# Layer 1's experts: second product feature-major with a gated input; layer 0's first loads on two queues

## What is computed

```python
raw_gate = jax.nn.softmax(x @ gate, axis=-1)                 # 16 experts
gate_topk = top 3 of raw_gate, divided by their sum           # 0 elsewhere
hidden = relu(einsum('btd,edh->bteh', x, W1) + b1)            # 128 -> 256
expert_out = einsum('bteh,ehd->bted', hidden, W2) + b2        # 256 -> 128
return einsum('bte,bted->btd', gate_topk, expert_out)
```

## Time and profile before

| what | us |
|---|---|
| median of three runs | 2104.19 |
| the profiled execution | 2104.40 |
| its span, first to last instruction | 2102.7 |
| layer 0, up to its last recurrence step | about 1164 |
| layer 1, experts by tiles | about 1178 to 1719 |
| attention | about 1719 to 2102.7 |
| TensorE busy, of the span | 1635.4 (78%) |
| VectorE | 1603.5 (76%) |
| ScalarE | 1137.1 (54%) |
| GpSimd | 1018.5 (48%) |

### The profile page before, as it was taken

One profiled execution on the slowest core, in us unless ns is written; L12 is line 12 of the kernel. 1 busy time (PEld: TensorE's weight loads), 2 busy tenths in 40 slices (PEclk: granted clock), 3 DMA queues, 4 the chain that ended last, 5 costly groups with the idle time before them and its releaser, 6 DMA issues. The chain is left out here.

```text
span 2102.7 us, 32686 instructions
## 1 busy us (share of the span) xinstructions
PE 1635.4 (78%) x8418; PEld 1185.5 (56%) x8418; DVE 1603.5 (76%) x4329; ACT 1137.1 (54%) x1811; POOL 1018.5 (48%) x1108
## 2 busy tenths in 40 slices
PE   3286787886868768778787399898999997888886
PEld 2164454554545436445454298787988875555554
DVE  3499999999999999999999535444344457777774
ACT  1365464564645646546454154444555447777774
POOL 2577778686787877887887400000000002332332
PEclk9598898897978988989898599999999999999998
DMA  5420020110200202002001411001110010000000
GB/s 83 108 56 1 1 66 1 25 43 1 66 0 4 63 2 51 15 0 61 1 11 38 103 21 26 19 14 27 21 26 11 11 31 9 15 22 15 22 15 13
DMA packets 140707, 58.82 MB, mean 28 GB/s; under 512 B 94743, under 2 KB 135180, under 8 KB 140556
## 3 DMA queue, kind: packets, MB, share of 16 engines
q1 hardware_dynamic: 140556, 57.19, 12.1%
HBM read 36.05 MB, written 21.10 MB: 27 GB/s over the span
## 5 line engine op out<-in xcount | busy, mean ns | idle before, releaser
L612 ACT ACTIVATE shared_rings<-pb 128x512 f32<-128x512 f32 (+1 forms) x784 | 434.7, 598 | 360.6 <-PE pb L639 318.4
L688 PE MATMUL pb<-hid,shared_down 128*128 128x512 f32 x528 | 308.0, 669 | 159.7 <-POOL hid L490 157.1
L486 POOL TENSOR_TENSOR hid<-shared_rings 128x512 f32<-128x512 f32 x256 | 333.9, 1304 | 178.6 <-ACT shared_rings L612 164.2
L490 POOL TENSOR_TENSOR hid<-hid,shared_rings 128x512 f32<-128x512 f32 x256 | 329.6, 1288 | 20.6 <-POOL hid L486 1.0
L1818 DVE SCALAR_TENSOR_TENSOR l_acc<-l_pb,l_gtok,l_acc 128x128 f32<-128x128 f32 x512 | 144.3, 344 | 256.1 <-PE l_pb L1462 256.1
L637 PE MATMUL pb<-xt_hi,shared_hi 128*128 128x512 f32 (+1 forms) x264 | 192.3, 729 | 101.6 <-ACT shared_rings L612 101.6
L1373 ACT ACTIVATE l_hid<-l_pb,l_cols 128x512 f32<-128x512 f32 x256 | 169.3, 688 | 182.8 <-PE l_pb L1462 182.5
L1462 PEld LDWEIGHTS l_pb<-l_big,l_hid 128*128 128x128 f32 x2048 | 247.1, 192 | 10.6
L1462 PE MATMUL l_pb<-l_big,l_hid 128*128 128x128 f32 x2048 | 247.9, 275 | 0.0
L1287 POOL TENSOR_TENSOR l_ql<-l_rope,l_qh 128x512 f32 x8 | 10.3, 1286 | 459.4 <-ACT l_qh L1367 459.4
L688 PEld LDWEIGHTS pb<-hid,shared_down 128*128 128x128 f32 x528 | 101.1, 207 | 217.0 <-POOL hid L490 191.3
(11 more groups left out here) (319 smaller groups left out, 3803.7 us busy)
## 6 DMA issues: line engine op xcount, KB each, us to landing
z_scratch<-zs SPq DMA_DIRECT2D x128, 81.0 KB, 3.0
zr<-z_scratch SPq DMA_DIRECT2D x8, 1296.0 KB, 8.0
x_sb<-in_L_attn_x_dram SPq DMA_DIRECT2D x32, 64.0 KB, 2.0
shared_rings<-in_L_ffn_We_gate_dram SPq DMA_DIRECT2D x4, 512.0 KB, 5.8
shared_rings<-in_L_ffn_We_up_dram SPq DMA_DIRECT2D x4, 512.0 KB, 6.9
g_scratch<-zs SPq DMA_DIRECT2D x8, 256.0 KB, 2.8
y_scratch<-yo SPq DMA_DIRECT2D x8, 256.0 KB, 2.1
shared_down<-in_L_ffn_W_dram SPq DMA_DIRECT2D x4, 512.0 KB, 5.6
```

The costliest lines, as they stand in the source:

```text
L486: pool.tensor_tensor(hid1[:, :], g, u, ALU.mult).then_inc(s_h1, 1)
L490: pool.tensor_tensor(hid[:, (p + par) % 2, :], hid1[:, :], c, ALU.mult).then_inc(s_h, 1)
L612: act.activation(dst, pb[0:n, what, :], ACT.Silu if what == 0 else ACT.Copy).then_inc(s_ev, 1)
L688: last = pe.matmul(pb[:, SUM, :], wd[0:n, p, :], hid[0:n, (p + par) % 2, :], start=(p == 0), stop=(p == PAIRS), skip_group_check=True)
```

## The change

1. Layer 1, second product. W2 is stationary and `hid` moves: output features by 512 tokens, one product per `r`, all 32 and the bias term summed in one PSUM bank (`summed`). For this the input is multiplied by the gate of its expert in place, by VectorE (`gated`), one 128x512 product for each `r`. The gate of an expert, a row over tokens, has to lie in all partitions: the transposed router weights `gT` are stored to DRAM, and SP loads two rows at a time to all 128 partitions (`gate_rows`, 512 KB, four buffers). A tile's sum goes through Silu, four transposes and a copy in the next tile (`silu`, `gate_out`). The second product lags the first by three rows (`LAG`); its last three stand in the next tile.
2. Layer 1, order. The query and key products, the rotary steps, the routing and the latent's Gelu are placed between the rows of the expert loop (`QK_AT`, `ROPE_AT`, `GELU_AT`, `DVE_AT`, ...). Tile 0 stands ahead of the loop, and the loop has three iterations again.
3. Queries and keys stay whole. Their split goes to attention: per batch one copy on ScalarE and one subtraction on GpSimd (`split_qk`), for the batch after the next.
4. Start of layer 0. Eight small loads go to ScalarE's queue, in two semaphores. The norm of tile 0 comes ahead of the weights' split on VectorE; the router's products come behind all projections, in a bank of their own; the last four stores of z are issued by ScalarE.

```diff
@@ SP and ScalarE, start of layer 0 @@
-            sp.dma_start(onehot[:, :], d["c_onehot"]).then_inc(s_small, 16)
...
+            for at, name in ((ZQ, "L0_attn_Wq"), (ZK, "L0_attn_Wk"), (ZV, "L0_attn_Wv")):
+                act.dma_start(wp[:, :, at:at + HD0], d[name].rearrange("i (h c) -> i h c", h=H0)).then_inc(s_heads, 16)
+            act.dma_start(wbeta[:, :], d["L0_attn_Wbeta"]).then_inc(s_heads, 16)
+            act.dma_start(gate_w[:, :], d["L0_ffn_gate_w"]).then_inc(s_late, 16)
...
@@ VectorE, start of layer 0 @@
-            for stage in range(6):
+            for stage in range(5):
                 layer_norm(0, 0, stage)
+            head_weights()
+            layer_norm(0, 0, 5)
+            dve.wait_ge(s_late, LATE * 16)
+            dve.tensor_copy(sel[:, :, :], over(onehot[:, :], F0)).then_inc(s_sel, 1)
...
@@ layer 1, places @@
+        R1 = 2 * E1
+        PE_AT = {0: "yT", 3: "mix", 12: "xT", 15: "router", 22: "gT"}
+        ACT_AT = {1: "yT", 6: "square", 9: "sqrt", 12: "xT", 17: "exp", 20: "kv", 22: "gT"}
+        DVE_AT = {2: "mix", 3: "centre", 6: "var", 8: "xn", 11: "xT", 14: "peak", 16: "softmax", 17: "top", 18: "gate"}
+        QK_AT, ROPE_AT, GELU_AT = (5, 8, 11, 14), (4, 7, 9, 13), (18, 19)
+        OUT_AT, SILU_AT, COPY_AT, SELECT_AT = 6, 4, 7, (22, 27)
...
@@ SP @@
+            def gate_rows(t, q, first):
+                if not first or q >= HELD:
+                    sp.wait_ge(s_mul, t * R1 + 4 * (q - HELD) + 4)
+                at = q % HELD
+                sp.dma_start(gates[:, 2 * at:2 * at + 2, :].rearrange("p q n -> p (q n)"),
+                             gT_dram[bass.ds(t, 1), 2 * q:2 * q + 2, :].rearrange("o e n -> o (e n)").to_broadcast([P, 2 * TOK])).then_inc(s_gate[at], 16)
+            def sp_tile(t, first, ahead, load):
+                gate_rows(t, HELD, first)
+                if ahead:
+                    keep_x2(t + 1)
+                gate_rows(t, HELD + 1, first)
+                if not first:
+                    keep_gate(t - 1)
+                if load:
+                    next_inputs(t + 2)
+                for q in range(HELD + 2, 2 * HELD):
+                    gate_rows(t, q, first)
+                if ahead:
+                    keep_gT(t + 1)
+                    for q in range(HELD):
+                        gate_rows(t + 1, q, False)
...
@@ GpSimd @@
-                    pool.wait_ge(s_qkh, t * 2 + (j + 1))
-                    pool.tensor_tensor(lo[:, :, at], rope[:, 2 * j, :].rearrange("p (b n) -> p b n", n=TP), hi[:, :, at].bitcast(F32), ALU.subtract).then_inc(s_qkl, 1)
+            def split_qk(b, par):
+                pool.wait_ge(s_qkh, b + 1)
+                both = qk[:, :, bass.ds(b, 1), :].rearrange("p j o n -> p j (o n)")
+                pool.tensor_tensor(qk_lo[par], both, qk_hi[par].bitcast(F32), ALU.subtract).then_inc(s_qkl, 1)
...
@@ TensorE, layer 1 @@
-                        for s in range(NS):
-                            for a in range(2):
-                                last = mm(pb[:, 5 + x % 2, sub[s]], hid[:, (2 * x + a) % HR, sub[s]], w2[:, x, a, :],
-                                          start=(a == 0), stop=(a == 1))
+            def summed(t, par, r):
+                pe.wait_ge(s_mul, t * R1 + (r + 1))
+                mm(pb[:, ACC + par, :], w2[:, r // 2, r % 2, :], hid[:, r % HR, :], start=False, stop=(r == R1 - 1)).then_inc(s_w2o, 1)
+            def tile(t, par, first, ahead):
+                for r in range(R1):
...
+                    if r in QK_AT:
+                        j = QK_AT.index(r)
+                        if j:
+                            pe.wait_ge(s_rope, t * ROPE + j)
+                        split3(pb[:, QK, :], wqk_hi[:, j, :], wqk_lo[:, j, :], hi, lo).then_inc(s_qk_ps, 1)
+                    hidden(t, par, r, first)
+                    if r < LAG:
+                        if not first:
+                            summed(t - 1, 1 - par, R1 - LAG + r)
+                    else:
...
+                        summed(t, par, r - LAG)
@@ VectorE, layer 1 @@
-                        dve.scalar_tensor_tensor(out=acc[:, s, :], in0=pb[:, 5 + e % 2, sub], scalar=gtok[par][:, s, e:e + 1],
-                                                 in1=acc[:, s, :], op0=ALU.mult, op1=ALU.add).then_inc(s_acc, 1)
+            def gated(t, r):
+                q = r // 4
+                if r % 4 == 0:
+                    dve.wait_ge(s_gate[q % HELD], t * 32 + 16 * (q // HELD + 1))
+                dve.wait_ge(s_hid, t * R1 + (r + 1))
+                row = hid[:, r % HR, :]
+                dve.tensor_tensor(row, row, gates[:, (r // 2) % (2 * HELD), :], ALU.mult).then_inc(s_mul, 1)
```

More of the change, by code:

```diff
@@ L675, in project, with router @@
                 last.then_inc(s_zp, 1)
+            def router(par, bank, first):
+                for s in range(NS):
+                    sub = slice(P * s, P * (s + 1))
+                    last = split3(bank[:, 256 + E0 * s:256 + E0 * (s + 1)], xt_hi[par][:, sub], xt_lo[par][:, sub], wr_hi[:, :], wr_lo[:, :], first=first and s == 0)
+                return last
             def router_weights(t):
@@ new lines, in hidden, with silu @@
+            def hidden(t, r, first):
+                act.wait_ge(s_w1o, t * R1 + (r + 1))
+                if not first or r >= HR:
+                    act.wait_ge(s_w2o, t * R1 + (r + 1 - HR))
+                act.activation(hid[:, r % HR, :], pb[:, 2 + r % 3, :], ACT.Relu, bias=cols[:, r:r + 1]).then_inc(s_hid, 1)
+            def silu(t, par):
+                act.wait_ge(s_w2o, t * R1 + R1)
+                act.wait_ge(s_g1st, t * (16 * BS))
+                act.activation(acc[:, :], pb[:, ACC + par, :], ACT.Silu).then_inc(s_silu, 1)
@@ L1377, in _ @@
-            for stage in ("yT", "square", "sqrt", "xT", "exp"):
+                    hidden(t, r, first)
+            front(0, 0, "yT")
+            for stage in ("square", "sqrt", "xT", "exp"):
                 front(0, 0, stage)
+            act.wait_ge(s_w1s, 4)
+            act.wait_ge(s_init, 10)
+            front(0, 0, "kv")
+            tile(0, 0, True, True)
             with act.Fori(0, NT // 2 - 1) as i:
-                tile(i * 2, 0, True)
-                tile(i * 2 + 1, 1, True)
@@ L1499, in front @@
                     last.then_inc(s_xt_ps, 1)
-                else:
+                elif stage == "router":
                     pe.wait_ge(s_xtl, t + 1)
@@ L1548, in _, with hidden @@
-            for stage in PE_AT.values():
+                else:
+                    pe.wait_ge(s_gt, t + 1)
+                    for s in range(NS):
+                        last = pe.transpose(pb[0:E1, 1, sub[s]], gtok[par][:, s, :], ident[:, :])
+                    last.then_inc(s_gT_ps, 1)
+            def hidden(t, par, r, first):
+                if r < 2 and not first:
+                    pe.wait_ge(s_hid, t * R1 + (r - 1))
+                elif r >= 3:
+                    pe.wait_ge(s_hid, t * R1 + (r - 2))
+                at = slice(P * r, P * (r + 1))
+                split3(pb[:, 2 + r % 3, :], w1_hi[:, at], w1_lo[:, at], xt[par][:, 0, :], xt[par][:, 1, :]).then_inc(s_w1o, 1)
@@ L1549, in _ @@
+            for stage in ("yT", "mix", "xT", "router"):
                 front(0, 0, stage)
+            pe.wait_ge(s_w1s, 4)
+            pe.wait_ge(s_w2, 32)
+            tile(0, 0, True, True)
             with pe.Fori(0, NT // 2 - 1) as i:
-                tile(i * 2, 0, True)
-                tile(i * 2 + 1, 1, True)
-            tile(NT - 2, 0, True)
-            tile(NT - 1, 1, False)
+                tile(i * 2 + 1, 1, False, True)
+                tile(i * 2 + 2, 0, False, True)
+            tile(NT - 1, 1, False, False)
@@ L1821, in tile @@
-            def tile(t, par, ahead):
-                turn(t)
-                experts(t, par, ahead)
-                if ahead:
-                    route(t + 1, 1 - par)
-            for stage in range(4):
-                mix(0, 0, stage)
-            centre(0)
-            route(0, 0)
+            def gated(t, r):
[5 more added lines that the diff above has]
+                dve.tensor_tensor(row, row, gates[:, (r // 2) % (2 * HELD), :], ALU.mult).then_inc(s_mul, 1)
@@ new lines, in tile @@
+            def tile(t, par, first, ahead):
+                for r in range(R1):
+                    if first and r == 0:
+                        for stage in ("softmax", "top", "gate"):
+                            front(0, 0, stage)
+                    if ahead and r in DVE_AT:
+                        front(t + 1, 1 - par, DVE_AT[r])
+                    if r in ROPE_AT:
+                        turn(t, ROPE_AT.index(r))
+                    if not ahead and r in SELECT_AT:
+                        selectors(SELECT_AT.index(r))
+                    gated(t, r)
@@ L1831, in _ @@
+            for stage in ("mix", "centre", "var", "xn", "xT", "peak"):
+                front(0, 0, stage)
+            tile(0, 0, True, True)
             with dve.Fori(0, NT // 2 - 1) as i:
```

(7 more changed lines are left out.)

481 lines of the change are left out of this document (256 added, 225 removed).

## The result

The changed kernel takes 2055.38 us (median of 4 runs, 2054.49 to 2055.6) beside 2105.56 us of the kernel before on the same chip (4 runs): ratio 0.9761, 95% interval 0.9744 to 0.9778. The profiled execution of the kernel after took 2054.49 us with a span of 2052.7.

| stretch | before, us | after, us | gain | forecast |
|---|---|---|---|---|
| to layer 1's first transposes (start of layer 0) | 1185.28 | 1174.40 | 10.9 | 15 |
| from there to the end of the last second product | 533.8 | 488.6 | 45.2 | 16.5 |
| attention | 383.7 | 389.7 | -6.0 | -3 |

A forecast was written before the change was run, and what follows sets the result against it. TensorE was taken to bound layer 1, idle at the tile seam, and VectorE layer 0. 2104.4 - 15 (start) - 16.5 (layer 1) + 2 + 1 (attention) = 2075.9, so 2076 us; range 2058 to 2093.

The forecast's parts named there:

- the selector row: Layer 1's gate loads, priced by the earlier profile's 512 KB selector load: 3.9 us each, hidden behind other work.
- Rival (a): Layer 1's expert pipeline has no stall worth naming: gain 25 to 28 us, time 2060 to 2066; chance 0.2.
- 8 x 60.5: Layer 1: eight steady tiles of 60.5 us TensorE work at full clock, against periods of 65.6 before.
- the price of a wide pass: Layer 1's second product: 0.461 us per 512-column pass from layer 0's down product; middle taken, 3.25 us per expert.
- 0.5 us of waits: Layer 1: TensorE waits 0.2 to 1 us per tile at VectorE and ScalarE inserts; 0.5 taken, 4 in all.
- The 5 us for the jumps: Layer 1's two remaining loop back edges cost 2.5 us each, 5 in all, bounds 0 and 10.
- the bound of 11: Start of layer 0: recurrence inputs come 15 us earlier, bounds 11 and 17.
- the long way: Start of layer 0: weight splitting inside the norm adds 2 us free, or 4 if its third step lasts 2.72.
- The split stores and the shorter path to the inputs: Start of layer 0: four stores on ScalarE's queue with less queueing 2 us; router passes off z's path net 2.
- the cast beside the subtraction: Attention: VectorE's small cast may wait for GpSimd's subtraction, 0.4 us per batch; +1 us taken, bounds 0 and 6.
- The entry: Start of attention: first product waits once for rectified silu, copy and split, +2 us (0 to 4).
- 28 us as the most that layer 1 could give: Layer 1's lower time bound: -28 us with no stall, no back edge and 1.70 us; -16.5 was forecast.

The follow-up runs named there:

- the experiment on the shape: Changed kernel with each second product cut into four passes of 128 columns instead of one of 512; ratio 0.9812 against the changed kernel's 0.9761.
- the written-out kernel: Kernel before with VectorE's loop over layer 1's tiles written out, other engines keeping their loops; ratio 0.9932 to the kernel before, 14 us less.
- the kernel with two rows of lag: Changed kernel with the second product two rows behind the first instead of three; ratio 0.99, 29 us more than the changed kernel.
- the experiment shows nothing for the stores: Changed kernel with all 16 stores of the first tile's projections on SyncE's queue, none on ScalarE's; ratio 0.9762, the same as the changed kernel.

## Why the prediction was right and wrong

**The bound and where the gain lies: right.** TensorE bounded layer 1 and the seam held its idle time; VectorE at 33 and ScalarE at 32 of 58 us are no bound (forecast: near 31 and near 32); the gate loads take 3.9 us as the selector row said and are never what VectorE waits for behind the first tile; the first second product came at 1216.7 (1216), though eight other traces have it up to 2.7 us later, so this hit is in part luck. Rival (a), 0.2, is what happened, and more of it. No kernel here has the new product without the new order or the other way round, so the split of layer 1's 45 us is an estimate: 9 for the wide shape (by the experiment), 13 for VectorE's jumps and the lower clocks (by the written-out kernel), and 25 for the seam's other idle time (63.0 - 59.9 us in each of eight tiles), 47 together.

**The term that failed is layer 1: 45.2 for 16.5 us.** Its sum was 8 x 60.5 with 10 us of waits, jumps and lower clock. Measured are 8 x 58.13, which is 19 us less, and none of the 9 us for waits and jumps: 28 of the 28.7 us. The 1 us for a lower clock was paid, and more: behind the stop of 3.00 us the work up to 1210.70 took 4.8 us, where the same passes take 3.1 at full clock. The step that failed first is the price of a wide pass, 0.461 us from the earlier trace rows. I subtracted a mean over the page (669 ns) from the length of one pair (1.13); in layer 1 the two passes of a pair stand 0.43 apart (1.02 less the 0.59 us of a single one). The clock was 1.00 around both pairs, so it is not what makes 1.13 of 1.02; the kernel with two rows of lag has 1.12 for the same pair where it begins behind a wait and 1.02 where it doesn't. And the row of the same stage showed the floor that I knew, 1.70 us per expert for the same columns. Taking the middle between a poor figure and a good one cost 0.14 us per expert, 2.2 us per tile, 18 in all; the experiment on the shape puts the true sign on it.

**The waits and jumps: 9 us that did not occur.** Per tile 0.5 us of waits was reasoned from a schedule that the slack of three rows covers; the kernel with two rows shows both that the detours are real and that the third row swallows them. The 5 us for the jumps stood on a row of another loop body: I took the gap of the earlier trace rows as a property of any jump, where it is one of the body's length. Its price in the kernel before, on the other side, was larger than I read there: 3.4 us, with 2.2 more of lower clock behind it.

**The start: 10.9 for 15, just below the bound of 11.** x was there at 5.88 (5), the first projection at 16.70 (15.2): 1.5 of the four. 0.9 of it is x, the other 0.6 that the splitting took the long way (its third step lasted 2.72 us again), where I had taken a middle. The split stores and the shorter path to the inputs were to give 4 together and gave 2.2 in these two traces (11.7 less 9.5); the experiment shows nothing for the stores, and the router's 12 passes took 2.5 us ahead of the first store in the kernel before, so they are the likely source of what was gained. The last 0.9 us went before layer 1 began. Over all traces this stage gives 10.7 us, just below the bound as here.

**Attention: -6 for -3.** Rows and place were named in the forecast (the cast beside the subtraction, 0 to 6); I took 1 us where fourteen batches paid 0.2 to 0.35 each, 4 in all; with the longer batches of either trace it is 3.2 from the first cast to the last (339.5 less 336.3). The entry cost the 2 us that were put down, and the last 0.4 us lie behind the last cast.

**The range.** Its low end rested on 28 us as the most that layer 1 could give, "no stall, no jump, 1.70 us". Added up from the forecast's own terms that case is 16.5 + 4 + 5 + 1 + 8 x 1.12 = 35.5 us, and the time 2057: the bound was cut short by an addition that was never made. The other 10 us of layer 1 are 8 x (59.4 - 58.13): at 1.70 a tile has 60.5 - 16 x 0.07 = 59.4 us, and the wide shape is cheaper than that by 1.2 (59.31 against 58.13 in the experiment). I had taken the old shape's cost as a floor for the new one, and nothing in the rows made it one.

## What to carry to other kernels

Price a pass from the stage in which it will run, at its clock, as start-to-start spacing; a mean over the page mixes stages, and "the middle" between it and a good row is an error shared by every tile. When a change removes the only stop of a saturated engine, its gain can be more than the stop: the lower clock behind it can go too. And before a loop's jump is charged to a new kernel, compare the length of the loop's body on that engine with the one that showed the gap.

## What the runs showed of the hardware that I had not expected

- The gap at a loop's end is one of single engines and comes with the length of the body: 2.4 to 3.3 us on VectorE with two tiles of 105 or 137 instructions, none with 73; on TensorE 1.2 and 1.6 us with two tiles of 407 products, none with 214.
- A stop of 4.5 to 4.8 us on TensorE was followed by the 1.2 GHz level in 4 of 4 cases, and the tile behind it was 2.2 us longer; stops of 1.4 to 1.8 us only in some, without a rule that these runs show.
- One fp32 product of 512 columns is 0.035 us cheaper than four of 128, though the columns are the same.
- Sixteen stores of 81 KB in the mean gained nothing from a second issuing queue: the load behind them came 18.2 us after the first projection with one, 17.3 to 19.4 with two (nine traces).
- A gate load's round trip in the open varies: the same store and load made TensorE wait 3.0 to 5.8 us in nine traces.
- A 128x32 cast on VectorE (0.20 us) lasted 0.45 us beside GpSimd's two-input subtraction and ended with it; with the subtraction moved it was 0.20 again.
